# Segment sums of gathered rows: chunks in pairs of a PSUM bank, and a ring of 96 chunks

## The chip, the cores and the metric

One core of one Trainium2 chip. The time is the device time of one execution in microseconds (us), the median of several. The engines are TensorE (PE in the profile), VectorE (DVE), ScalarE (ACT), GpSimd (POOL) and SyncE (SP), which issues most transfers.

## The reference, cut to what matters

```python
# x (50000, 128) float32; src, dst (100000,), dst sorted: 50000 random edges and a loop at each node
h_self = x @ W_self.T + b_self
messages = x[src] @ W_neigh.T + b_neigh
h_neigh = segment_sum(messages, dst, num_segments=50000)
out = layernorm(x + relu(h_self + h_neigh))      # eps 1e-5, no affine part
```

The kernel sums rows of x first and multiplies once per node. An edge's loop part needs no gather, so 50,000 edges are left, and the count of a node's edges multiplies b_neigh.

## The kernel before, in words

**Lists.** The 50,000 edges that are no loops are packed in 391 chunks of 128, in the order of dst. Vector makes, from the edge lists, for each chunk the source nodes (chunk_src), the targets (chunk_dst) and the first target (first_node). They come in three parts of 99, 99 and the rest, the later two in slices between the other work (later_lists(t) of Vector): chunk_src of part 2 at t = 11 and of part 3 at t = 39. GpSimd waits for a part before it gathers from it (L466 to L475).

**Gathers.** GpSimd issues one indirect DMA a chunk (L462), in order; it brings 128 rows of x into a slot of `ring`, 84 slots. From chunk 84 on it waits (L461) until TensorE has summed triple (c - 84)//3 + 2: a triple is three chunks, and the last row block of a triple is read again by the next triple's carry matmul.

**Sums.** For a chunk Vector builds `pick` (L724), a one-hot matrix of edges by node columns; TensorE multiplies the gathered rows with it (L889), which gives the sum per node, transposed, features by nodes. A triple shares one PSUM bank of 496 columns, with chunks over columns 0 to 192, 64 to 344 and 168 to 496, so 800 columns are multiplied a triple (two matmul records in the trace for each float32 matmul). A node whose edges go on in the next triple gets the rest by a matmul of one column, the carry (L883). ScalarE copies the bank's 496 columns into `sums_t` (L990), a ring of 4096 node columns with a margin, at an offset read from a list into a register; copies overlap in columns, so each waits for the one before it. Vector joins the margin with the start at each lap (L742, L743) and clears it (L748).

**Nodes.** Nodes are worked in 131 trios of 3 x 128, counted by tau. TensorE transposes x (turn_x, L873), ScalarE copies it (L998), TensorE adds bias (L904), x times W_self + W_neigh (L908) and sums_t times W_neigh (L909) in a bank. Vector takes relu and adds x (residual, L735), and makes the statistics (L755, L763, L771, L778); ScalarE the deviation (L1007) and the scaling (L1017). SP loads x and degrees and stores the result, each with four buffers.

**Order.** Each engine has its program written out, without loops on the device. TensorE, for each t: the sums up to what sums_needed(t) says and one triple more (L946), turn_x(t + 1), products(t). products(t) waits for sums_placed, xt_copied and y_done. ScalarE, for each t: place_sums as far as TensorE sums, copy_x_t(t + 1), deviation(t - 2), normalise(t - 3). Vector, for each t: residual(t - 1), joins, the picks for t + 1, statistics, the lists. How many triples products(t) needs follows from `drift_of`, the bound on how far a chunk's first node may lie from an even spread: 768 nodes, and 384 near both ends. Inputs that break a bound go to a second, general program (check, conclude), which these inputs don't need.

Of the kernel before, what the change touches and what calls it, by code (L numbers as in the profile page):

```python
# [20 lines left out]
INT32 = mybir.dt.int32  # L21
# [4 lines left out]
P = 128  # L26
# [35 lines left out]
SPANS = ((0, 192), (64, 344), (168, 496))  # L62
SPAN = SPANS[-1][1]
PICK_AT = (0, 192, 472)
PICK = 800
# [39 lines left out]
def drift_of(triple):  # L105
    return DRIFT if TIGHT_LOW < triple < TIGHT_HIGH else TIGHT_DRIFT


def sums_needed(trio):

    return 1 + max(c for c in range(TRIOS) if P * TRIO * c - drift_of(c) < P * TRIO * (trio + 1))


def lap_joined_after(lap):

    return 1 + max(c for c in range(TRIOS) if P * TRIO * c - drift_of(c) < lap * LAP)
# [7 lines left out]
def lap_reused_from(lap):  # L124

    return -(-((lap + 1) * LAP - DRIFT - SPAN + 1) // (P * TRIO))

# [44 lines left out]
def build_common_case(nc, ctx, k, x, src, dst, out):  # L172
# [55 lines left out]
    carry = sb("carry", [P, TRIOS])  # L228
    offset_all = sb("offset_all", [1, ENTRIES // TRIO], INT32)
    offsets = sb("offsets", [1, ENTRIES // TRIO + LOAD], INT32)  # L230
# [7 lines left out]
    expected = sb("expected", [1, TRIOS])  # L238
    gap = sb("gap", [1, CHUNKS])
    faults = sb("faults", [1, 10])  # L240
# [19 lines left out]
    sum_bank, xt_bank, h_bank, list_bank = bank[0:3], bank[3:5], bank[5:7], bank[7]  # L260
# [33 lines left out]
    triples_summed = sem("triples_summed")  # L294
    sums_placed = sem("sums_placed")
    laps_joined = sem("laps_joined")
# [33 lines left out]
    with nc.Block() as block_:  # L330
# [75 lines left out]
        def _(pool):  # L406
# [8 lines left out]
            iota(columns[:], [[1, SPAN]], 0).then_inc(k.iotas, 1)  # L415
            iota(expected[:], [[TRIO * P, TRIOS]], 0).then_inc(k.iotas, 1)
# [38 lines left out]
            def gather(c):  # L455
# [4 lines left out]
                if c >= RING:  # L460
                    pool.wait_ge(triples_summed, (c - RING) // TRIO + 2)  # L461
# [16 lines left out]
        def _(dve):  # L478
# [142 lines left out]
            def spread_lists(part, t0, t1, carry0, carry1):  # L621

                c0, c1 = t0 * TRIO, t1 * TRIO
                dve.wait_ge(firsts_spread, part)
                link(v.tensor_copy(first_node[:, c0:c1], list_bank[:, 0:c1 - c0]))
                v.tensor_copy(offset_all[:, t0:t1], first_node[0:1, c0:c1:TRIO])
                v.tensor_tensor(carry[:, carry0:carry1], chunk_dst[:, carry0 * TRIO + TRIO - 1:carry1 * TRIO:TRIO],
                                first_node[:, (carry0 + 1) * TRIO:carry1 * TRIO + 1:TRIO], ALU.is_equal)
                link(v.tensor_tensor(local[:, c0:c1].rearrange("p (t q) -> p t q", q=TRIO),
                                     chunk_dst[:, c0:c1].rearrange("p (t q) -> p t q", q=TRIO),  # L630
                                     first_node[:, c0:c1:TRIO].unsqueeze(2).to_broadcast([P, t1 - t0, TRIO]), ALU.subtract))
                link(v.scalar_tensor_tensor(local[:, carry0 * TRIO + TRIO - 1:carry1 * TRIO:TRIO], carry[:, carry0:carry1], float(LAP),
                                            local[:, carry0 * TRIO + TRIO - 1:carry1 * TRIO:TRIO], ALU.mult, ALU.add))
                v.tensor_scalar(offsets[:, t0:t1], offset_all[:, t0:t1], LAP - 1, None, ALU.bitwise_and).then_inc(offsets_known, 1)
# [26 lines left out]
            spread_lists(1, 0, FIRST_TRIOS, 0, FIRST_TRIOS - 1)  # L661
# [19 lines left out]
            def check():  # L681
# [4 lines left out]
                firsts = first_node[0:1, 0:TRIOS * TRIO + 1]  # L686
                starts = firsts[:, 0:TRIOS * TRIO:TRIO]
                link(v.tensor_tensor(gap[:], firsts[:, 1:CHUNKS + 1], firsts[:, 0:CHUNKS], ALU.subtract))
                count(0, gap[:], LONGEST, ALU.is_gt)
                link(v.tensor_tensor(gap[:, 0:TRIOS - 1], firsts[:, 1:(TRIOS - 1) * TRIO:TRIO], starts[:, 0:TRIOS - 1], ALU.subtract))  # L690
                count(1, gap[:, 0:TRIOS - 1], SPANS[1][0], ALU.is_lt)
                link(v.tensor_tensor(gap[:, 0:TRIOS - 1], firsts[:, 2:(TRIOS - 1) * TRIO:TRIO], starts[:, 0:TRIOS - 1], ALU.subtract))
                count(2, gap[:, 0:TRIOS - 1], SPANS[2][0], ALU.is_lt)
                count(3, gap[:, 0:TRIOS - 1], SPANS[1][1] - 1, ALU.is_gt)
                link(v.tensor_tensor(gap[:, 0:TRIOS], firsts[:, TRIO:TRIOS * TRIO + 1:TRIO], starts, ALU.subtract))
                count(4, gap[:, 0:TRIOS], SPAN - 1, ALU.is_gt)
                link(v.tensor_tensor(gap[:, 0:TRIOS - 1], firsts[:, TRIO:(TRIOS - 1) * TRIO + 1:TRIO], firsts[:, 2:(TRIOS - 1) * TRIO:TRIO], ALU.subtract))
                count(5, gap[:, 0:TRIOS - 1], 1, ALU.is_lt)
                link(v.tensor_tensor(gap[:, 0:TRIOS], starts, expected[:], ALU.subtract))
                count(6, gap[:, 0:TRIOS], DRIFT, ALU.is_gt)  # L700
                count(7, gap[:, 0:TRIOS], -DRIFT, ALU.is_lt)
                count(8, gap[:, 0:TIGHT_LOW + 1], -TIGHT_DRIFT, ALU.is_lt)
                count(9, gap[:, TIGHT_HIGH:TRIOS], -TIGHT_DRIFT, ALU.is_lt)
                link(v.tensor_copy(unused[:, 0:10], faults[:]))
                v.reduce_sum(checks[0:1, 1:2], unused[:, 0:10], AXIS_X)
# [11 lines left out]
            def build_picks(tau):  # L717

                if tau >= DEEP:
                    dve.wait_ge(triples_summed, tau - DEEP + 1)  # L720
                for c in chunks_of(tau):
                    q = c % TRIO
                    lo, hi = SPANS[q]
                    ins = v.tensor_scalar(pick[tau % DEEP][:, PICK_AT[q]:PICK_AT[q] + hi - lo], columns[:, lo:hi],  # L724
                                          local[:, c:c + 1], None, ALU.is_equal)
                ins.then_inc(pick_built, 1)
# [54 lines left out]
            def later_lists(t):  # L781
# [13 lines left out]
                if t == 13:  # L795
                    spread_lists(2, FIRST_TRIOS, 2 * FIRST_TRIOS, FIRST_TRIOS - 1, 2 * FIRST_TRIOS - 1)
# [18 lines left out]
                if t == 41:  # L815
                    spread_lists(3, 2 * FIRST_TRIOS, ENTRIES // TRIO, 2 * FIRST_TRIOS - 1, TRIOS - 1)
# [16 lines left out]
            for t in range(TRIOS + 2):  # L833
# [22 lines left out]
        def _(pe):  # L856
# [9 lines left out]
            def turn_x(tau):  # L866
                b = tau % 2
                tiles, rows = tiles_of(tau)
                pe.wait_ge(x_landed[tau % DEEP], 16 * (tau // DEEP + 1))
                if tau >= 2:  # L870
                    pe.wait_ge(xt_copied, tau - 1)
                for q in range(tiles):
                    ins = nc.tensor.transpose(xt_bank[b][:, q * P:q * P + rows], x_in[tau % DEEP][0:rows, q, :], k.identity[0:rows, 0:rows])  # L873
                ins.then_inc(xt_turned, 1)

            def sum_chunks(tau):

                sums = sum_bank[tau % SUM_BANKS]
                pe.wait_ge(pick_built, tau + 1)
# [391 lines left out]
```

## Time and profile before

| | |
|---|---|
| median of 3 runs | 803.71 us (801.73 to 805.24) |
| the profiled execution | 807.21 us |
| its span in the profile | 805.3 us |
| mean granted TensorE clock | 0.87 of full speed |
| busy | PE 548.5, DVE 446.5, ACT 303.8, POOL 405.0 us |

The profile is of one execution. "L904" is a line of the kernel. A wait is given with what released it; "remote", or "another core or an unknown queue", stands where the trace shows no releaser, and "issue" where it shows no wait. PE is the matrix work, PEld the load of weights beside it.

### The profile page before, as it was taken

The page shows a single profiled execution, that of the slowest core. Times are in us where ns is not written, and L with a number is a line of the kernel's source. Part 1 is how long each engine was busy: PE and PEld are TensorE (multiplying, and loading weights), DVE is VectorE, ACT ScalarE, POOL GpSimd, SP SyncE. Part 2 cuts the span into 40 slices and gives each one's busy share as a digit, 9 for nine tenths or more (in the row PEclk, how much of TensorE's full clock was granted, in tenths as well). Part 3 has the DMA queues.
Part 4 walks back from the last instruction along what each step waited for, and adds up shares of the span by engine and source line. Part 5 has one row for each costly group of instructions (what it writes and reads, how often), then busy time and mean ns, then how long its engine had stood idle before and what let it go on. Part 6 is the DMA issues. An engine that isn't in the chain of part 4 may idle for free.

```text
span 805.3 us, 11397 instructions
## 1 busy us (share of the span) xinstructions
PE 548.5 (68%) x3151; PEld 434.5 (54%) x3151; DVE 446.5 (55%) x1927; ACT 303.8 (38%) x789; POOL 405.0 (50%) x424
## 2 busy tenths in 40 slices
PE   1036020118941879889678787888989798999995
PEld 0024010016730657677456576666767576778784
DVE  6783001008821768689566666675645455666765
ACT  0000000015501444446244354435445354566566
POOL 3687777731176556562756566556656566200000
PEclk9999555558985799999879999889979899999998
DMA  4222222113331435444334444434544444433333
GB/s 136 62 63 65 53 52 62 52 27 92 102 83 52 113 103 145 125 129 128 93 93 132 119 122 110 126 110 132 133 110 129 129 126 129 122 109 101 112 107 93
DMA packets 122933, 82.12 MB, mean 102 GB/s; under 512 B 15374, under 2 KB 115894, under 8 KB 122840
## 3 DMA queue, kind: packets, MB, share of 16 engines
q1 hardware_dynamic: 109208, 53.63, 23.5%
q0 software_dynamic: 13664, 27.77, 13.6%
q8 instruction: 26, 0.43, 0.2%
q14 instruction: 35, 0.29, 0.1%
HBM read 55.44 MB, written 26.71 MB: 102 GB/s over the span
## 4 chain that ended last, share of the span: by engine, by line
PE 41%; issue 21%; DVE 15%; another core or an unknown queue 11%; ACT 6%; POOL 4%; DMA 2%; ACTq 1%; DVEq 0%; POOLq 0%
PE bank L889 17%; PE bank L908 8%; PE bank L909 7%; DVE pick L724 4%; PE bank L873 4%; ACT result L1017 3%; PE bank L904 3%; DVE y L735 2%; PE bank L883 2%; DVE stats L755 2%; ACT sums_t L990 1%; POOL ring L462 1%; DMA dst_block<-in_dst,block_index 1%; POOL dst_block L422 1%
## 5 line engine op out<-in xcount | busy, mean ns | idle before, releaser
L462 POOL DMA_INDIRECT ring<-in_x,chunk_src x391 | 379.9, 972 | 265.7 <-issue 110.2
L990 ACT COPY sums_t<-bank 128x496 f32 x131 | 74.9, 572 | 415.5 <-remote 223.1
L889 PE MATMUL bank<-pick,ring 128*128 128x192 f32 (+2 forms) x782 | 227.6, 431 | 2.4 <-DMA ring<-in_x,chunk_src 2.4
L908 PE MATMUL bank<-wsum_t,x_t 128*128 128x128 f32 (+1 forms) x782 | 173.2, 304 | 11.7 <-issue 11.5
L735 DVE SCALAR_TENSOR_TENSOR y<-bank,x_in 128x384 f32<-128x384 f32 x131 | 72.5, 554 | 191.5 <-PE bank L909 73.9
L909 PE MATMUL bank<-wn_t,sums_t 128*128 128x128 f32 (+1 forms) x782 | 158.6, 284 | 19.4 <-issue 19.4
L1017 ACT ACTIVATE result<-y,minus_mean,rstd 128x128 f32<-128x128 f32 x391 | 163.4, 486 | 0.0
L889 PEld LDWEIGHTS bank<-pick,ring 128*128 128x128 f32 x782 | 142.5, 205 | 17.1 <-DMA ring<-in_x,chunk_src 1.9
L908 PEld LDWEIGHTS bank<-wsum_t,x_t 128*128 128x128 f32 (+1 forms) x782 | 124.8, 200 | 37.7 <-issue 37.7
L909 PEld LDWEIGHTS bank<-wn_t,sums_t 128*128 128x128 f32 (+1 forms) x782 | 125.5, 201 | 18.9 <-issue 18.9
L724 DVE TENSOR_SCALAR pick<-columns,local 128x192 f32<-128x192 f32 (+2 forms) x391 | 118.0, 357 | 0.2
L883 PE MATMUL bank<-carry,ring 128*128 128x1 f32 x260 | 43.6, 237 | 86.4 <-DVE pick L724 62.9
L883 PEld LDWEIGHTS bank<-carry,ring 128*128 128x128 f32 x260 | 41.9, 201 | 98.4 <-DVE pick L724 71.6
L904 PE MATMUL bank<-bias,degrees_t 12*128 12x384 bf16 x131 | 45.4, 346 | 71.5 <-issue 61.2
L771 DVE RECIPROCAL rstd<-std 128x3 f32<-128x3 f32 x131 | 21.9, 167 | 127.5 <-issue 75.1
L755 DVE BATCH_NORM_STATS2 stats<-y 128x6 f32<-128x128 f32 x391 | 87.4, 278 | 0.2
L998 ACT COPY x_t<-bank 128x384 f32<-128x384 f32 x131 | 63.1, 482 | 61.7 <-PE bank L873 34.8
L873 PE MATMUL bank<-identity,x_in 128*128 128x128 f32 x391 | 70.3, 289 | 18.8 <-issue 18.8
L873 PEld LDWEIGHTS bank<-identity,x_in 128*128 128x128 f32 x391 | 54.8, 150 | 49.5 <-issue 24.4
L904 PEld LDWEIGHTS bank<-bias,degrees_t 12*128 12x128 bf16 x131 | 12.0, 91 | 99.0 <-issue 98.8
L1007 ACT ACTIVATE std<-mean_var,eps 128x3 f32<-128x3 f32 x131 | 40.2, 307 | 0.4 <-DVE mean_var L763 0.4
L763 DVE BATCH_NORM_AGGREGATE mean_var<-stats 128x2 f32<-128x6 f32 x391 | 38.9, 155 | 0.0
(122 smaller groups left out, 208.8 us busy)
## 6 DMA issues: line engine op xcount, KB each, us to landing
x_in<-in_x SPq DMA_DIRECT2D x130, 192.0 KB
out<-result SPq DMA_DIRECT2D x130, 192.0 KB
ring<-in_x,chunk_src POOLq DMA_INDIRECT x391
degrees_t<-degrees_dram SPq DMA_DIRECT2D x130, 2.2 KB
dst_padded<-in_dst SPq DMA_DIRECT2D x1, 390.6 KB
src_padded<-in_src SPq DMA_DIRECT2D x1, 390.6 KB
edge_src<-in_src SPq DMA_DIRECT2D x1, 390.6 KB
edge_dst<-in_dst SPq DMA_DIRECT2D x1, 390.6 KB
```

What stands on the lines that cost most here:

```text
L462: nc.gpsimd.indirect_dma_start(ring[:, c % RING, :], None, x, bass.IndirectOffsetOnAxis(ap=chunk_src[:, c:c + 1], axis=0)).then_inc(gather ...
L724: ins = v.tensor_scalar(pick[tau % DEEP][:, PICK_AT[q]:PICK_AT[q] + hi - lo], columns[:, lo:hi], local[:, c:c + 1], None, ALU.is_equal)
L735: v.scalar_tensor_tensor(y[tau % DEEP][0:rows, 0:tiles, :], h_bank[b][0:rows, 0:tiles * DIM].rearrange("p (q d) -> p q d", q=tiles), 0.0, ...
L755: ins = v.bn_stats(stats[b][0:rows, q, :], y[b][0:rows, q, :])
L873: ins = nc.tensor.transpose(xt_bank[b][:, q * P:q * P + rows], x_in[tau % DEEP][0:rows, q, :], k.identity[0:rows, 0:rows])
L883: mm(sums[:, 0:1], ring[:, (tau * TRIO - 1) % RING, :], carry[:, tau - 1:tau], start=True, stop=False, skip_group_check=True)
L889: ins = mm(sums[:, lo:hi], ring[:, c % RING, :], pick[tau % DEEP][:, PICK_AT[q]:PICK_AT[q] + hi - lo], start=(tau == 0 and q == 0), stop=( ...
L904: mm(h_bank[b][0:rows, 0:tiles * DIM], degrees_t[tau % DEEP][:, 0:rows], k.bias[:, 0:tiles, :], start=True, stop=False)
L908: mm(h, x_t[b][:, q, 0:rows], k.wsum_t[:], start=False, stop=False)
L909: ins = mm(h, sums_t[:, at:at + rows], k.wn_t[:], start=False, stop=(q == tiles - 1))
L990: nc.scalar.copy(sums_t[:, bass.ds(at, SPAN)], sum_bank[tau % SUM_BANKS][:, 0:SPAN]).then_inc(sums_placed, 1)
L1017: ins = nc.scalar.activation(result[b][0:rows, q, :], y[b][0:rows, q, :], ACT.Identity, bias=minus_mean[b][0:rows, q:q + 1], scale=rstd[b] ...
```

## The change

A chunk now has 193 columns of its own, at its own offset, and two chunks lie side by side in one bank: columns 0 to 192 and 192 to 384, the shared column 192 being the first of the second chunk. An edge whose target is the next chunk's first node goes to column 192 of its chunk. The second chunk's last column (384) is added to the first column of the next chunk in sums_t by an activation of ScalarE with that column as its bias, after the next chunk's copy. The carry matmul is gone, but not `carry`, from which `local` is made. Picks are three of 194 columns a trio. place_sums runs once a chunk (391 times) and copies 192 columns; register loads bring 8 offsets each. The ring of gathered rows has 96 slots, and gather c waits for chunks_summed of c - 95, so that chunk c - 96 has been summed; each chunk's matmul increments that semaphore. Four banks hold sums, one holds transposed x (before three and two), so turn_x waits for the copy of the transposes before. The sums run ahead of products(t) by what it needs and at least two chunks more, in whole pairs. The drift bounds are 640, 384 and 192 nodes. The margin of sums_t is 192 columns. The checks on the lists are changed to match.

```diff
-SPANS = ((0, 192), (64, 344), (168, 496))
-SPAN = SPANS[-1][1]
+SPAN = 192
+PAIR = 2
...
-MARGIN = 512
+MARGIN = SPAN
...
-DRIFT = 768
+DRIFT = 640
 TIGHT_DRIFT = 384
-TIGHT_LOW = 14
-TIGHT_HIGH = 117
-
-RING = 84
+END_DRIFT = 192
+TIGHT_CHUNKS = 42
+END_CHUNKS = 9
+
+RING = 96
 GATHER_SEMS = 8
-SUM_BANKS = 3
-LOAD = 4
+SUM_BANKS = 4
+LOAD = 8
...
+def drift_of(chunk):
+    from_end = min(chunk, CHUNKS - chunk)
+    return END_DRIFT if from_end <= END_CHUNKS else TIGHT_DRIFT if from_end <= TIGHT_CHUNKS else DRIFT
+
+def chunks_starting_below(node):
+    return 1 + max(c for c in range(CHUNKS) if P * c - drift_of(c) < node)
+
+def whole_pairs(chunks):
+    return min(CHUNKS, -(-chunks // PAIR) * PAIR)
 
 def sums_needed(trio):
-    return 1 + max(c for c in range(TRIOS) if P * TRIO * c - drift_of(c) < P * TRIO * (trio + 1))
+    return chunks_starting_below(P * TRIO * (trio + 1))
+
+def sums_ahead(trio):
+    return whole_pairs(sums_needed(min(trio, TRIOS - 1)) + PAIR)
...
-    columns = sb("columns", [P, SPAN])
+    columns = sb("columns", [P, SPAN + 2])
...
-    pick = [sb(f"pick{i}", [P, PICK]) for i in range(DEEP)]
+    pick = [sb(f"pick{i}", [P, TRIO, SPAN + 2]) for i in range(DEEP)]
...
-    sum_bank, xt_bank, h_bank, list_bank = bank[0:3], bank[3:5], bank[5:7], bank[7]
+    sum_bank, xt_bank, h_bank, list_bank = bank[0:4], bank[4], bank[5:7], bank[7]
...
                 if c >= RING:
-                    pool.wait_ge(triples_summed, (c - RING) // TRIO + 2)
+                    pool.wait_ge(chunks_summed, c - RING + 1)
...
-                link(v.scalar_tensor_tensor(... float(LAP), ... ALU.mult, ALU.add))
+                link(v.scalar_tensor_tensor(local[:, r0:r1], carry[:, r0:r1], float(SPAN), local[:, r0:r1], ALU.mult, ALU.max))
...
                 if tau >= DEEP:
-                    dve.wait_ge(triples_summed, tau - DEEP + 1)
+                    dve.wait_ge(chunks_summed, TRIO * (tau - DEEP + 1))
                 for c in chunks_of(tau):
...
+                    ins = v.tensor_scalar(pick[tau % DEEP][:, c % TRIO, :], columns[:], local[:, c:c + 1], None, ALU.is_equal)
...
-                while built < min(TRIOS, sums_needed(min(t + 1, TRIOS - 1)) + 1):
+                while built * TRIO < sums_ahead(t + 1):
...
-                if tau >= 2:
-                    pe.wait_ge(xt_copied, tau - 1)
+                if tau >= 1:
+                    pe.wait_ge(xt_copied, tau)
...
-            def sum_chunks(tau):
...
-                if tau:
-                    mm(sums[:, 0:1], ring[:, (tau * TRIO - 1) % RING, :], carry[:, tau - 1:tau], start=True, stop=False, skip_group_check=True)
...
+            def sum_chunk(c):
+                tau = c // TRIO
+                if c % TRIO == 0:
+                    pe.wait_ge(pick_built, tau + 1)
+                    pe.wait_ge(gathered[tau % GATHER_SEMS], gathers_upto(tau))
+                frame = SPAN * (c % PAIR)
+                into = sum_bank[c // PAIR % SUM_BANKS]
+                if c % PAIR == 0 and c // PAIR >= SUM_BANKS - 1:
+                    pe.wait_ge(sums_placed, PAIR * (c // PAIR + 2 - SUM_BANKS))
+                ins = mm(into[:, frame:frame + SPAN + 1], ring[:, c % RING, :], pick[tau % DEEP][:, c % TRIO, 0:SPAN + 1],
+                         start=(c % PAIR == 0), stop=True, skip_group_check=True)
+                ins.then_inc(chunks_summed, 1)
...
-                while summed < min(TRIOS, sums_needed(t) + 1):
-                    sum_chunks(summed)
+                while summed < sums_ahead(t):
+                    sum_chunk(summed)
...
+            def place_sums(c):
+                if c % LOAD == 0:
+                    load_offsets(c)
+                at = act.snap(held[c % LOAD], min_val=0, max_val=LAP - 1)
+                if c % PAIR == 0:
+                    act.wait_ge(chunks_summed, min(c + PAIR, CHUNKS))
...
+                    act.wait_ge(sums_placed, c)
...
+                frame = SPAN * (c % PAIR)
+                whole = sum_bank[c // PAIR % SUM_BANKS]
+                copied = nc.scalar.copy(sums_t[:, bass.ds(at, SPAN)], whole[:, frame:frame + SPAN])
+                if c > 0 and c % PAIR == 0:
+                    copied.then_inc(frames_copied, 1)
+                    act.wait_ge(frames_copied, c // PAIR)
+                    nc.scalar.activation(sums_t[:, bass.ds(at, 1)], sum_bank[(c // PAIR - 1) % SUM_BANKS][:, PAIR * SPAN:PAIR * SPAN + 1],
+                                         ACT.Identity, bias=sums_t[:, bass.ds(at, 1)], scale=1.0).then_inc(sums_placed, 1)
+                else:
+                    copied.then_inc(sums_placed, 1)
...
-                while placed < min(TRIOS, sums_needed(min(t, TRIOS - 1)) + 1):
+                while placed < sums_ahead(t):
```

## Rows read from the trace of the kernel before

**Rows 1.** The page's busy times: us, share of the span, instructions.

```profile
PE 548.5 (68%) x3151; PEld 434.5 (54%) x3151; DVE 446.5 (55%) x1927; ACT 303.8 (38%) x789; POOL 405.0 (50%) x424
```

**Rows 2.** Stretches, L904: length, busy us (and instructions) on PE and weight load, clock, DMA.

```profile
184.30:218.40 34.10, 2.71 (x8) 0.73 (x8) 0.93 0.38 106
...
218.40:259.40 41.00, 0.86 (x3) 0.28 (x3) 0.73 0.26 71
...
382.10:691.50 309.40, 21.17 (x61) 5.55 (x61) 0.91 0.44 119
...
691.50:805.30 113.80, 9.85 (x30) 2.72 (x30) 0.98 0.38 107
```

**Rows 3.** Stretches, L462 on POOL: length, busy us (gathers), clock, DMA share, GB/s.

```profile
218.40:259.40 41.00, 31.12 (x33) 0.73 0.26 71
...
382.10:691.50 309.40, 185.80 (x193) 0.91 0.44 119
```

**Rows 4.** Timeline, 606 to 612: start, us taken, engine, line, form [idle before].

```profile
606.43 0.39 PE L909 MATMUL bank<-wn_t,sums_t 128*128 128x128 f32 x2
...
606.80 1.59 PE L889 MATMUL bank<-pick,ring 128*128 128x192 f32 x6
...
608.00 0.94 POOL L462 DMA_INDIRECT ring<-in_x,chunk_src  x1 [0.30 <-issue]
...
610.48 0.56 DVE L735 SCALAR_TENSOR_TENSOR y<-bank,x_in 128x384 f32<-128x384 f32 x1 [3.29 <-remote]
...
610.65 0.57 ACT L990 COPY sums_t<-bank 128x496 f32 x1 [2.76 <-remote]
...
611.31 1.05 POOL L462 DMA_INDIRECT ring<-in_x,chunk_src  x1 [2.37 <-remote]
```

**Rows 5.** POOL's waits, 382 to 691.5: us in total, times, longest.

```profile
POOL ring L462 <- remote: 47.1, 22, 4.4
...
POOL ring L462 <- PE bank L889: 24.6, 12, 4.7
```

**Rows 6.** Timeline of PE in the tail, one trio.

```profile
718.10 0.28 PE L883 MATMUL bank<-carry,ring 128*128 128x1 f32 x2
...
718.24 1.59 PE L889 MATMUL bank<-pick,ring 128*128 128x192 f32 x6
...
719.67 0.49 PE L873 MATMUL bank<-identity,x_in 128*128 128x128 f32 x3
...
720.09 0.33 PE L904 MATMUL bank<-bias,degrees_t 12*128 12x384 bf16 x1
...
721.80 0.28 PE L883 MATMUL bank<-carry,ring 128*128 128x1 f32 x2
```

**Rows 7.** Timeline of ACT in the tail, one trio.

```profile
719.95 0.57 ACT L990 COPY sums_t<-bank 128x496 f32 x1 [1.41 <-PE bank L889]
720.42 0.49 ACT L998 COPY x_t<-bank 128x384 f32<-128x384 f32 x1
720.79 0.31 ACT L1007 ACTIVATE std<-mean_var,eps 128x3 f32<-128x3 f32 x1
720.98 1.25 ACT L1017 ACTIVATE result<-y,minus_mean,rstd 128x128 f32<-128x128 f32 x3
```

**Rows 8.** Forms of ACT in the tail, and of DVE: busy us, mean ns, idle before.

```profile
L1007 ACT ACTIVATE std<-mean_var,eps 80x1 f32<-80x1 f32 x1 | 0.3, 280 | 0.0
...
L998 ACT COPY x_t<-bank 128x80 f32<-128x80 f32 x1 | 0.2, 210 | 0.0
...
L742 DVE TENSOR_TENSOR sums_t<-sums_t 128x512 f32<-128x512 f32 x12 | 8.3, 688 | 13.7 <-ACT sums_t L990 13.7
...
L743 DVE MEMSET sums_t<- 128x512 f32 x12 | 5.8, 485 | 2.1 <-DVE sums_t L742 1.6 <-issue 0.5
```

**Rows 9.** Timeline: the gathers after two stops, and PE before the first.

```profile
181.34 0.57 PE L909 MATMUL bank<-wn_t,sums_t 128*128 128x128 f32 x1 [0.34 <-issue]
...
184.33 0.94 POOL L462 DMA_INDIRECT ring<-in_x,chunk_src  x1 [14.75 <-remote]
...
382.17 0.94 POOL L462 DMA_INDIRECT ring<-in_x,chunk_src  x1 [12.67 <-DVE chunk_dst L657]
```

More of the change, by code:

```diff
@@ L102, in gnn_kernel @@
             build_general_case(nc, general, weights, x, src, dst, out)
-def drift_of(triple):
-    return DRIFT if TIGHT_LOW < triple < TIGHT_HIGH else TIGHT_DRIFT
+def drift_of(chunk):
[5 more added lines that the diff above has]
+    return min(CHUNKS, -(-chunks // PAIR) * PAIR)
 def sums_needed(trio):
-    return 1 + max(c for c in range(TRIOS) if P * TRIO * c - drift_of(c) < P * TRIO * (trio + 1))
+    return chunks_starting_below(P * TRIO * (trio + 1))
+def sums_ahead(trio):
+    return whole_pairs(sums_needed(min(trio, TRIOS - 1)) + PAIR)
 def lap_joined_after(lap):
-    return 1 + max(c for c in range(TRIOS) if P * TRIO * c - drift_of(c) < lap * LAP)
+    return chunks_starting_below(lap * LAP)
 def lap_read_by(lap):
@@ L124, in lap_reused_from @@
 def lap_reused_from(lap):
-    return -(-((lap + 1) * LAP - DRIFT - SPAN + 1) // (P * TRIO))
+    return -(-((lap + 1) * LAP - DRIFT - SPAN + 1) // P)
 class Constants:
@@ L227, in build_common_case @@
     local = sb("local", [P, ENTRIES])
-    carry = sb("carry", [P, TRIOS])
-    offset_all = sb("offset_all", [1, ENTRIES // TRIO], INT32)
-    offsets = sb("offsets", [1, ENTRIES // TRIO + LOAD], INT32)
+    carry = sb("carry", [P, ENTRIES])
+    offset_all = sb("offset_all", [1, ENTRIES], INT32)
+    offsets = sb("offsets", [1, ENTRIES + LOAD], INT32)
     raw_at = sb("raw_at", [SPREAD, WINDOW])
@@ L691, in check @@
[L691 to L696, printed above, removed]
@@ L866, in turn_x @@
             def turn_x(tau):
[L867 removed]
                 tiles, rows = tiles_of(tau)
                 pe.wait_ge(x_landed[tau % DEEP], 16 * (tau // DEEP + 1))
[L870 to L871 removed]
+                if tau >= 1:
+                    pe.wait_ge(xt_copied, tau)
                 for q in range(tiles):
[L873 removed]
+                    ins = nc.tensor.transpose(xt_bank[:, q * P:q * P + rows], x_in[tau % DEEP][0:rows, q, :], k.identity[0:rows, 0:rows])
                 ins.then_inc(xt_turned, 1)
[L876 to L891 removed]
+            def sum_chunk(c):
[10 more added lines that the diff above has]
+                ins.then_inc(chunks_summed, 1)
             def products(tau):
@@ L972, in place_sums @@
[L972 to L978 removed]
+                act.load(held[:], offsets[:, c:c + LOAD])
+            def place_sums(c):
[4 more added lines that the diff above has]
+                    act.wait_ge(chunks_summed, min(c + PAIR, CHUNKS))
+                if c == 0:
@@ L988, in place_sums @@
                 if free_of >= 0:
                     act.wait_ge(h_done, free_of + 1)
-                nc.scalar.copy(sums_t[:, bass.ds(at, SPAN)], sum_bank[tau % SUM_BANKS][:, 0:SPAN]).then_inc(sums_placed, 1)
+                frame = SPAN * (c % PAIR)
[8 more added lines that the diff above has]
+                    copied.then_inc(sums_placed, 1)
```

93 lines of the change are left out of this document (32 added, 61 removed).

## The prediction, made before the changed kernel was run

> **What bounds the kernel now.** I read the page's shares first, then the span in stages, then one stretch of each kind. The page shows no full engine: TensorE is busy 68%, GpSimd 50%, ScalarE 38% [rows 1]. So no share settles it, and a saving on one engine buys nothing by itself.
>
> Cut at GpSimd's gathers, the span shows three kinds of stage. The number of bias matmuls (L904, one per trio) against the number of gathers tells them apart [rows 2, 3]:
> - GpSimd runs without a stop. In 218.4 to 259.4 it issues 33 gathers and TensorE starts 3 trios. The stretch before the first stop is alike.
> - GpSimd is held by the ring. In 382.1 to 691.5 there are 193 gathers and 61 trios, 5.07 us a trio; the stretch from 259 to the wait for the third list is of this kind too.
> - GpSimd is idle: 30 trios in the last 113.8 us, and 8 in 184.3 to 218.4, where it waits for the second list.
>
> Why the middle stage is slow shows at 606 to 612 [rows 4]. The products end at 606.82, but Vector's residual, which waits for them, starts at 610.48. The sums end at 608.39 and ScalarE's copy starts at 610.65. GpSimd has ended its last allowed gather at 608.94 and resumes at 611.31, 2.37 later. So the consumers hear of TensorE's work late, about 1.5 us after GpSimd has stopped, and all at once. I cannot name the mechanism from the trace; I take the pattern: while gathers run one behind the other, what TensorE has finished is seen late, and a stop of GpSimd frees it. In the middle stage there are 34 such stops, 71.7 us, so 2.1 us each and 5.7 gathers between two [rows 5]. A gather takes 0.94 us and has 0.30 before it, 1.25 from start to start [rows 4], so a stop costs 1.8 us more than going on. That is cheap: 1.8 us of a stopped GpSimd lets TensorE do nearly two trios, which in the tail take 7.4 us.
>
> With GpSimd idle the beat is 3.70 us, and it is TensorE's: carry 0.14, sums 1.43, transposes 0.42, bias and products 1.71 (from the starts at 718.10, 718.24, 719.67, 720.09 and 721.80) [rows 6]. ScalarE waits 1.41 of it [rows 7].
>
> **TensorE's saving.** Sums go from 800 columns to 3 x 193 = 579 a trio: 1.43 x 579/800 = 1.03, and the carry's 0.14 goes. 3.70 becomes 3.17. Where TensorE doesn't set the beat this is worth nothing.
>
> **ScalarE's cost.** One copy of 496 columns becomes three of 192 and, for each pair, one add of a column. Each waits for the one before it, and the add for its copy. A copy of 192 lies between the 0.21 us of 80 columns and the 0.49 of 384, 0.31 us on that line [rows 7, 8]. The one-column activation with a bias pointer from PSUM isn't in the trace; the 80x1 activation takes 280 ns [rows 8], and the 128x128 with two pointers 0.48 (three in 1.25, from start to start 0.385) [rows 7]; I take 0.28, the nearest form. From a releasing instruction's end to the next copy takes 0.12 us (the sums end at 719.83, the copy starts at 719.95) [rows 6, 7]. So 3 x 0.43 + 1.5 x 0.40 = 1.89 us. The rest of its trio is 1.73: 0.37 from the copy of x to the deviation, 0.19 to the scaling, and 1.16, three by 0.385, for that [rows 7]. Less 0.1 of overlap, ScalarE needs 3.5 us a trio, more than TensorE's 3.17. Ends: 3.25 if the waits cost 0.07, 3.9 if the add costs 0.48 and the waits 0.15. So the idle-GpSimd beat becomes 3.5, not 3.17: a gain of 0.18 us.
>
> The Trainium skill (ScalarE: Activation LUTs, What ACT_TABLE_LOAD costs) gives 186 ns and 0.833 ns an element with immediates, and 93 ns more for a pointer. By it the copy is 0.35, the add 0.28, and the beat an estimated 3.6; the sum would rise by about 6 us.
>
> **The ring.** It grows from 84 to 96 chunks, and its release is finer. Gather c now waits for chunk c-96; before, since a trio's last row was also read by the next trio's carry, it waited for triple (c-84)/3+2. The last gather (390) needs 104 triples summed before, 312 chunks, and 295 chunks after. The lookahead of the sums is 4 triples before (L946) and 3t+10 chunks, rounded up to a pair, after. So GpSimd ends when trio 100 is in work before (which the counts bear out: 30 bias matmuls are left after 691.5 [rows 2]) and trio 95 after. Gather 197 allows trio 35 before, 31 after. A longer lead is not a gain here: GpSimd has the same 391 gathers to issue at 1.25, and every trio put off until it is idle costs 3.5, where in the middle stage it costs only its share of a stop, 1.8/2.
>
> Step by step, against the profiled execution (807.21 us, span 805.3, which lies 0.4% over the median 803.71):
> - First list: the 14.75 us stop at gather 96 goes [rows 9], but then GpSimd waits for the second list, which needs Vector at t = 11. TensorE came free 12 us after the last gather (169.58, and 181.91 for the last of the products) [rows 9]; three more gathers put that off by 4 us. Bounds 0 and +8, I take +2.
> - Second list: 8 trios at 3.5 for 3.7: -1.4.
> - To gather 198: 4.3 trios fewer are worked before it, 2.2 stops less, -4.3. Then GpSimd waits for the third list, which Vector makes at t = 39: 12.67 us now [rows 9], and 4.3 x 3.5 = 15.1 more, less 0.6 for the quicker beat. Together +10.2.
> - Middle stage: 5 trios fewer, 2.6 stops: -4.7.
> - Tail: 5 trios more at 3.5, +17.6; 30 trios by 0.18 less, -5.5; 12.1 together.
> - Laps' joins: 512 to 192 columns, 0.69 us for the add of each of 12 [rows 8]; perhaps 0.1 us a lap is seen, -1.
>
> Sum: 2 - 1.4 + 10.2 - 4.7 + 12.1 - 1 = +17 us. That gives 824 for a profiled execution, and **821 us** against the median.
>
> Nothing: the picks (582 columns for 800) can only shorten Vector's part, which is hidden by its waits; without that cover the sign is still a gain. One transpose bank for two: its copy is done a whole trio before. The lists' larger spread is some columns more, beside the gathers; if seen, under 1 us. Loads of offsets, one per 8 chunks: beside the scaling; without that cover 0.3 us each, already in the upper beat. SP's queue and GpSimd's issues keep their number; SP's loads and stores wait for the same events. ScalarE's scaling stands behind the longer placing, and the store behind that, with four buffers between.
>
> **Rivals.**
> 1. *More chunks per stop, and TensorE's beat* (the other side). The release is by chunk and TensorE's trio is shorter, so a third trio may fit between two stops. Some 208 chunks are worked in ring-held stages; at 8 a stop for 5.7 that is 208 x 1.8 x (1/5.7 - 1/8) = 19 us less, 802. If the chain on ScalarE also hides, 51 trios (35 + 8 + 8) run at 3.17: another 17, 785. For: TensorE's two trios take 7.4 us of the 9.5 between two restarts of GpSimd (7.5 for six gathers, 2.1 for the stop), so it has room. Against: products need the pair just summed in every other trio, where before they needed only the trio before. It decides from 8 chunks a stop together with a beat under 3.4. Chance 0.25 for 775 to 799, 0.11 for one half of it, near 803.
> 2. *Fewer chunks per stop.* If the pair that products need is heard only at a stop, GpSimd stops every 4 chunks: 208 x 1.8 x (1/4 - 1/5.7) = +28, 849. Chance 0.08.
> 3. *ScalarE's chain at its upper bound*: 3.9 by 51 trios, +20, 841. It's part of my case's range.
> 4. *TensorE's bound everywhere*: 131 x 0.53 = 69 us less, 735. The middle stage, in which TensorE is not the limit, speaks against it: 0.02, within the 0.25.
>
> **How the numbers follow.** My case (lead dearer than the beat's gain) has 0.56 and spans 806 to 845; with rival 2, slower by over 0.5%, which is about what a measurement of this kernel can tell from no change, gets 0.64. Faster 0.25, within 0.5% 0.11. The range reaches from most of rival 1 to the lower part of rival 2: 784 to 848. My own case's stands above.
>
> **What would show it.** Right: the last gather issued near 695 to 702 with 34 to 36 trios left; a wait of 25 to 30 us before gather 198; L883 gone, sums of a trio near 1.03 us at full clock; in the tail a beat of 3.4 to 3.6, ScalarE without idle time and TensorE waiting for sums_t. Wrong: a tail beat of 3.2 with ScalarE idle; a wait before gather 198 no longer than 15 us; stops in the middle stage fewer than 20 or more than 45.

## The result, and the profile after

| | before | changed |
|---|---|---|
| median of 4 runs | 804.48 us (801.73 to 806.39) | 817.24 us (814.21 to 821.50) |
| ratio, 95% interval | | 1.0178 [1.0138, 1.0218] |
| the profiled execution, its span | 807.21, 805.3 us | 817.83, 815.9 us |
| mean granted TensorE clock | 0.87 | 0.82 |

The change made the kernel 1.8% slower, which is clear of the spread of the runs; 821.0 was predicted, in a range of 784 to 848. Medians and ratios are of fast runs: two of e4's four runs (733.73 and 734.53 us) were in a slower state and are left out. In the changed kernel L478 is the gather, L887 the sums, L991 the copy of a chunk's columns, L995 the added column, L902 the bias matmul (one per trio), L1006, L1015 and L1025 ScalarE's other three steps, L744 and L745 the laps' join.

The page's busy times and groups of the changed kernel (busy us, mean ns | idle before), which answer to [rows 1]:

```profile
PE 480.2 (59%) x2891; PEld 401.4 (49%) x2891; DVE 418.6 (51%) x1919; ACT 397.9 (49%) x1244; POOL 407.4 (50%) x424
...
L991 ACT COPY sums_t<-bank 128x192 f32 x391 | 124.1, 317 | 318.9 <-remote 202.5
L887 PE MATMUL bank<-pick,ring 128*128 128x193 f32 x782 | 171.8, 353 | 55.0 <-issue 41.8
...
L995 ACT ACTIVATE sums_t<-bank,sums_t 128x1 f32 x195 | 51.0, 261 | 6.3
```

TensorE lost 68 us of work and ScalarE gained 94, and the time moved by 13: busy times settle nothing here. The stretches do, cut at GpSimd's stops as in [rows 2, 3]. First L902: length, busy us (and instructions) on PE and on the weight load, granted clock, DMA share, GB/s.

```profile
221.00:281.20 60.20, 1.13 (x3) 0.28 (x3) 0.58 0.25 71
...
396.70:691.70 295.00, 19.79 (x55) 5.06 (x55) 0.85 0.43 118
691.70:815.90 124.20, 11.48 (x35) 3.19 (x35) 0.97 0.41 115
```

In 221.0 to 281.2 GpSimd issues 48 gathers without a stop, and TensorE starts 3 trios. The middle stage has the same 193 gathers as before, with 55 trios for 61. The last gather goes at 691.7, as before, but 35 trios are left instead of 30. GpSimd's timeline at the two list waits and at the end (start, us taken, engine, line, form, [idle before]), which answers to [rows 9]:

```profile
221.05 0.94 POOL L478 DMA_INDIRECT ring<-in_x,chunk_src  x1 [47.80 <-DVE chunk_dst L669]
...
396.77 0.95 POOL L478 DMA_INDIRECT ring<-in_x,chunk_src  x1 [30.41 <-DVE chunk_dst L669]
...
691.69 0.95 POOL L478 DMA_INDIRECT ring<-in_x,chunk_src  x1 [0.30 <-issue]
```

The first list wait, 47.80, stands where there were two before: the stop of 14.75 at gather 96 and one of 30.46 for the list, so the stop only moved. The wait before gather 198 was 12.67. So of the span's 10.6 us more, 14.6 were there by gather 198 (396.8 against 382.2), the middle stage gave 14.4 back (295.0 against 309.4), and the tail took 10.4 more (124.2 against 113.8). GpSimd's waits in the middle stage (us in total, times, longest), which answer to [rows 5]:

```profile
POOL ring L478 <- PE bank L887: 34.6, 25, 2.7
...
POOL ring L478 <- remote: 26.7, 21, 2.1
```

61.3 us in 46 stops, 1.33 each, for 71.7 in 34, 2.1 each. Above the ordinary gap of 0.30 that is 0.25 us per gather ((61.3 - 46 x 0.30)/193), for 0.32 before. The stops come more often and are cheaper. (The counts go by the releaser that the trace names, and some of these waits are of the ordinary length. Counted by length, over 0.36 us, there are 43 stops of 1.42 us for 37 of 2.06: six more, not twelve.)

ScalarE in the tail, for two trios (the last lines of the second, from its fourth copy on, are left out), which answers to [rows 7]:

```profile
730.32 0.31 ACT L991 COPY sums_t<-bank 128x192 f32 x1
730.66 0.26 ACT L995 ACTIVATE sums_t<-bank,sums_t 128x1 f32 x1
731.03 0.32 ACT L991 COPY sums_t<-bank 128x192 f32 x1
731.25 0.48 ACT L1006 COPY x_t<-bank 128x384 f32<-128x384 f32 x1
731.62 0.31 ACT L1015 ACTIVATE std<-mean_var,eps 128x3 f32<-128x3 f32 x1
731.82 1.26 ACT L1025 ACTIVATE result<-y,minus_mean,rstd 128x128 f32<-128x128 f32 x3
732.97 0.30 ACT L991 COPY sums_t<-bank 128x192 f32 x1
733.31 0.26 ACT L995 ACTIVATE sums_t<-bank,sums_t 128x1 f32 x1
733.68 0.32 ACT L991 COPY sums_t<-bank 128x192 f32 x1
734.15 0.32 ACT L991 COPY sums_t<-bank 128x192 f32 x1 [0.15 <-ACT sums_t L991]
734.50 0.26 ACT L995 ACTIVATE sums_t<-bank,sums_t 128x1 f32 x1
...
736.81 0.30 ACT L991 COPY sums_t<-bank 128x192 f32 x1
```

It is idle for 0.15 us in 6.49, where it waited 1.41 in 3.70. The trios alternate: one has two copies and an add and takes ScalarE 2.65 (730.32 to 732.97), the other four and two and takes 3.84 (to 736.81). TensorE's side of the same trios, which answers to [rows 6]:

```profile
731.41 1.47 PE L887 MATMUL bank<-pick,ring 128*128 128x193 f32 x8
732.73 0.49 PE L874 MATMUL bank<-identity,x_in 128*128 128x128 f32 x3
733.72 0.32 PE L902 MATMUL bank<-bias,degrees_t 12*128 12x384 bf16 x1 [0.50 <-ACT sums_t L995]
...
735.41 0.82 PE L887 MATMUL bank<-pick,ring 128*128 128x193 f32 x4
...
736.49 0.33 PE L902 MATMUL bank<-bias,degrees_t 12*128 12x384 bf16 x1
...
740.21 0.32 PE L902 MATMUL bank<-bias,degrees_t 12*128 12x384 bf16 x1 [0.22 <-ACT sums_t L995]
```

From one bias matmul to the next it is 2.77 us where two chunks are summed between (TensorE's own time) and 3.72 where four are (it waits for ScalarE's add). Over the tail, without its last two intervals (which have no work of other trios in them), the mean is 3.38. The joins fell as their columns did (busy us, mean ns; groups of DVE by line), for 688 and 485 in [rows 8]:

```profile
L744 DVE TENSOR_TENSOR sums_t<-sums_t 128x192 f32<-128x192 f32 x12 | 4.3, 359 | 8.7 <-ACT sums_t L995 5.6 <-issue 3.1
L745 DVE MEMSET sums_t<- 128x192 f32 x12 | 2.6, 218 | 1.3
```

### The profile page after: what moved, and what is told of

The parts are those of the page before. It is cut to its first block, busy times and chain, and to the rows that moved or that the text cites. A ratio compares the mean times of both kernels' runs of the same rounds, so it can differ in the third digit from the quotient of the medians.

```text
span 815.9 us, 12095 instructions
## 1 busy us (share of the span) xinstructions
PE 480.2 (59%) x2891; PEld 401.4 (49%) x2891; DVE 418.6 (51%) x1919; ACT 397.9 (49%) x1244; POOL 407.4 (50%) x424
## 4 chain that ended last, share of the span: by engine, by line
PE 29%; another core or an unknown queue 27%; ACT 16%; issue 12%; DVE 8%; POOL 3%; ACTq 2%; DMA 2%; DVEq 0%; POOLq 0%
PE bank L887 9%; PE bank L906 8%; PE bank L907 6%; ACT result L1025 6%; ACT sums_t L991 5%; PE bank L874 3%; PE bank L902 3%; ACT sums_t L995 2%; DVE pick L727 2%; ACT x_t L1006 1%; ACT std L1015 1%; DVE y L737 1%; DMA dst_block<-in_dst,block_index 1%; ACTq L988 1%
## 5 line engine op out<-in xcount | busy, mean ns | idle before, releaser
L478 POOL DMA_INDIRECT ring<-in_x,chunk_src x391 | 383.1, 980 | 262.6 <-issue 101.2
L991 ACT COPY sums_t<-bank 128x192 f32 x391 | 124.1, 317 | 318.9 <-remote 202.5
L887 PE MATMUL bank<-pick,ring 128*128 128x193 f32 x782 | 171.8, 353 | 55.0 <-issue 41.8
L906 PE MATMUL bank<-wsum_t,x_t 128*128 128x128 f32 (+1 forms) x782 | 181.7, 318 | 0.0
L887 PEld LDWEIGHTS bank<-pick,ring 128*128 128x128 f32 x782 | 137.0, 207 | 65.6 <-issue 49.6
L907 PE MATMUL bank<-wn_t,sums_t 128*128 128x128 f32 (+1 forms) x782 | 166.8, 298 | 0.3 <-issue 0.3
L1025 ACT ACTIVATE result<-y,minus_mean,rstd 128x128 f32<-128x128 f32 x391 | 163.4, 486 | 0.0
L906 PEld LDWEIGHTS bank<-wsum_t,x_t 128*128 128x128 f32 (+1 forms) x782 | 132.4, 212 | 26.6 <-issue 26.6
L907 PEld LDWEIGHTS bank<-wn_t,sums_t 128*128 128x128 f32 (+1 forms) x782 | 134.1, 215 | 0.0
L902 PE MATMUL bank<-bias,degrees_t 12*128 12x384 bf16 x131 | 46.2, 353 | 143.2 <-issue 98.8
L727 DVE TENSOR_SCALAR pick<-columns,local 128x194 f32<-128x194 f32 x391 | 103.3, 320 | 0.2
L1006 ACT COPY x_t<-bank 128x384 f32<-128x384 f32 x131 | 63.1, 481 | 68.5 <-remote 36.1
L902 PEld LDWEIGHTS bank<-bias,degrees_t 12*128 12x128 bf16 x131 | 12.0, 92 | 169.6 <-issue 169.4
L995 ACT ACTIVATE sums_t<-bank,sums_t 128x1 f32 x195 | 51.0, 261 | 6.3
L1015 ACT ACTIVATE std<-mean_var,eps 128x3 f32<-128x3 f32 x131 | 40.2, 307 | 0.0
L597 DVE COPY_PREDICATED words<-moves,words 99x311 int32<-99x311 int32 (+15 forms) x48 | 27.2, 566 | 1.1
```

The costliest lines, as they stand in the source:

```text
L478: nc.gpsimd.indirect_dma_start(ring[:, c % RING, :], None, x, bass.IndirectOffsetOnAxis(ap=chunk_src[:, c:c + 1], axis=0)).then_inc(gather ...
L727: ins = v.tensor_scalar(pick[tau % DEEP][:, c % TRIO, :], columns[:], local[:, c:c + 1], None, ALU.is_equal)
L887: ins = mm(into[:, frame:frame + SPAN + 1], ring[:, c % RING, :], pick[tau % DEEP][:, c % TRIO, 0:SPAN + 1], start=(c % PAIR == 0), stop=T ...
L902: mm(h_bank[b][0:rows, 0:tiles * DIM], degrees_t[tau % DEEP][:, 0:rows], k.bias[:, 0:tiles, :], start=True, stop=False)
L906: mm(h, x_t[b][:, q, 0:rows], k.wsum_t[:], start=False, stop=False)
L907: ins = mm(h, sums_t[:, at:at + rows], k.wn_t[:], start=False, stop=(q == tiles - 1))
```

## The experiments

The prediction claims two things: the longer lead of the gathers (more slots, and release by chunk) costs more than the rest of the change brings, and with GpSimd idle the chain on ScalarE eats most of what TensorE saves. The experiments ran in four groups, each with the kernel before on the same chip, and each ratio below is to that one: 804.24 us (e1 to e4), 581.2 (e5 to e7), 803.58 (e8 to e10), 808.78 (e11, e12). The 581.2 is a matter of its own, told below, and e5 to e7 aren't in the table. The columns on gathers and trios are read from one trace of each kernel (e4's is of its run of 733.73 us); gather 198 is left out where no wait for a list stands before it.

| kernel | slots, release | gather 198 at | last gather | trios left | rest of the span | median us | ratio |
|---|---|---|---|---|---|---|---|
| before | 84, triple | 382.2 | 691.5 | 30 | 113.8 | 804.48 | |
| e3 | 96, triple | 400.3 | 701.7 | 34 | 131.3 | 834.73 | 1.038 |
| changed | 96, chunk | 396.8 | 691.7 | 35 | 124.2 | 817.24 | 1.018 |
| e8, the same again | 96, chunk | 397.5 | 698.3 | 35 | 123.5 | 823.78 | 1.024 |
| e9, e8 without the add | 96, chunk | 394.2 | 689.1 | 35 | 115.0 | 805.82 | 1.004 |
| e1 | 79, chunk | 374.2 | 673.2 | 29 | 104.0 | 777.39 | 0.967 |
| e2 | 48, chunk | | 649.6 | 19 | 70.1 | 719.00 | 0.893 |
| e4 | 48, triple | | 663.4 | 18 | 68.5 | 724.99 | 0.902 |
| e11 | 24, chunk | | 669.3 | 10 | 39.9 | 710.14 | 0.881 |
| e12 | 12, chunk | | 668.6 | 6 | 25.6 | 698.06 | 0.867 |

**e1: the changed kernel with the old lead.** With 79 slots and release by chunk, the last gather needs 312 chunks summed, the same as before.

```diff
-RING = 96
+RING = 79
```

> The changed kernel with 79 slots in the ring instead of 96, nothing else. With a release by chunk this gives the last gather the same lead as the kernel before (312 chunks summed). Theory (a longer lead costs, since trios put off until GpSimd is idle cost a full beat): 5.7 trios fewer stand behind the last gather, 5.7 x 3.38 = 19 us less tail; the wait before gather 198 falls from 30 to about 11 us; about 8 us more in stops. Together -30 us: 787, under the kernel before. Rival (the change's loss is ScalarE's longer placing, and the ring is neutral): within 5 us of the changed kernel's 817. Second rival (a longer lead helps, as it saves stops): 825.

777.39 us, 0.9665 [0.9624, 0.9705]: 40 us under the changed kernel, where 30 was expected. So at the old lead everything else in the change is worth 27 us, and the seventeen slots cost 40. (Two gathers in three wait in e1 for one or two chunks more than in the kernel before, so its lead is shorter by one chunk in the mean; at 40 us for seventeen that is an estimated 2 of the 27.) The stretches of e1 (L902), cut at gather 198 and at the last:

```profile
374.10:673.30 299.20, 21.45 (x61) 5.61 (x61) 0.89 0.45 125
673.30:777.20 103.90, 9.54 (x29) 2.65 (x29) 0.94 0.41 114
```

The 28 us of span less than before lie in all three parts: 8 by gather 198 (374.2 for 382.2), 10 in the middle stage, 10 in the tail. The terms of the prediction that have nothing to do with the lead add up to 8.5 (1.4, 0.6, 5.5 and 1).

**e3: the kernel before with 96 slots,** and nothing else.

```diff
-RING = 84
+RING = 96
```

> The kernel before with 96 slots instead of 84: the ring's part of the change alone. Theory: 4 trios more behind the last gather and behind gather 197, 2 x 4 x 3.7 = 30 us more, less 8 us of stops: 826. Rival (the ring is neutral or helps): 804 or less.

834.73 us (826 expected), 1.0381 [1.0339, 1.0422]: 30 us slower, by a longer prefetch alone. GpSimd's waits of e3 up to the last gather:

```profile
POOL ring L462 <- DVE chunk_dst L657: 78.1, 2, 49.7
POOL ring L462 <- remote: 59.5, 25, 7.9
POOL ring L462 <- PE bank L889: 28.0, 18, 3.5
```

The two waits for lists are 49.7 and 28.4 us. In its tail 34 trios are left and the bias matmuls stand 3.70 apart, TensorE's beat as before. This is the prediction's mechanism by itself: the same gathers are issued, and the trios that were put off are worked one by one while GpSimd has nothing to do.

**e2 and e4: both kernels with 48 slots.**

In e2, the changed kernel (in e4, the kernel before, the old value is 84):

```diff
-RING = 96
+RING = 48
```

> The changed kernel with 48 slots. Theory: GpSimd is held by the ring from gather 48 on, both list waits vanish, and the tail falls to some 19 trios: 47 us ahead of the first gather, 489 us of gathers, 81 us of stops, 68 us of tail, 685 us, between 650 and 715. Rival (the ring neutral): 817. Second rival (a short ring starves TensorE, since gathers land late or the lists come late): over 817.

> The kernel before with 48 slots. Theory: as for the changed kernel with 48, with stops of 2.1 us and a tail beat of 3.7: 47 + 489 + 110 + 66 = 712 us, between 680 and 740. Rival (neutral): 804. It also says whether the changed kernel is the faster one once the lead is short: by theory it is, by some 25 us.

719.00 us, 0.8932 [0.8888, 0.8975], and 724.99 us (of two runs), 0.9022 [0.8967, 0.9076]. The direction held and the size fell short: a little over the range in e2, within it in e4. The other half of e4's expectation missed: with 48 slots the changed kernel was to be faster by some 25 us, and it is by 6, with intervals that overlap. So what the rest of the change is worth isn't a fixed sum; it depends on the ring it stands beside. GpSimd's waits of e2:

```profile
POOL ring L478 <- PE bank L887: 84.2, 58, 3.1
POOL ring L478 <- remote: 43.6, 29, 8.5
```

No wait for a list is left (78 us in the changed kernel), but the stops are 127.8 us in 87, where I had expected 81. Less 26 for the ordinary gaps, that is 0.26 us per gather over all 391, the price per gather of the changed kernel's middle stage. It is now paid from the first stop to the end. The span falls by 96 us: 42 before the last gather (649.6 for 691.7) and 54 in the tail.

**e5 to e7: a chip on which the kernel before takes 581 us.** e5 leaves out the add of a pair's last column (the sums of the nodes at a pair's end lack it), e6 is the changed kernel with 24 slots, e7 replaces the indirect gathers by plain transfers of 128 rows (the sums are of other rows; what the gathers bring is left out).

```diff
-                if c > 0 and c % PAIR == 0:
-                    copied.then_inc(frames_copied, 1)
...
-                                         ACT.Identity, bias=sums_t[:, bass.ds(at, 1)], scale=1.0).then_inc(sums_placed, 1)
-                else:
-                    copied.then_inc(sums_placed, 1)
+                copied.then_inc(sums_placed, 1)
```

```diff
-                nc.gpsimd.indirect_dma_start(ring[:, c % RING, :], None, x,
-                                             bass.IndirectOffsetOnAxis(ap=chunk_src[:, c:c + 1], axis=0)
+                nc.gpsimd.dma_start(ring[:, c % RING, :], x[P * min(c, TILES - 2):P * min(c, TILES - 2) + P, :]
                                     ).then_inc(gathered[tau % GATHER_SEMS], 16)
```

> The changed kernel with the add of a pair's last column left out (those nodes' sums lack a part); 96 slots. Theory (with GpSimd idle the beat alternates between TensorE's and ScalarE's, and the chain of copies and adds is what keeps it at 3.38 us instead of 3.17): 1.5 x 0.38 us of ScalarE go per trio, the tail's beat falls to TensorE's, 2.8 to 3.2 us, over some 51 trios that are worked while GpSimd is idle: 10 to 15 us less, 802 to 807. Rival (the chain is hidden, the beat is TensorE's own): within 3 us of 817.

> The changed kernel with 24 slots. Theory (only the lead and the stops count): against 48 slots the tail is 8 trios shorter, 8 x 3.2 = 26 us, with 24/4.6 = 5 stops more of 1.2 us, 6 us: 719 - 20 = 699. Rival (with so few slots the time from a gather's issue to its landing, or the pairs' grain, starves TensorE): over 719.

> The changed kernel with each gather replaced by a plain transfer of 128 rows of x of the same size, issued by GpSimd too (so the sums are of other rows). It asks what delays the hearing of TensorE's work. If the indirect gathers' descriptors on GpSimd do it, the late starts and the stops' 1.2 us vanish, TensorE works through the early stretch, and the time falls well under 750. If it is GpSimd's issuing of any transfer, or the traffic itself, it stays above 790.

567.31 us (0.9781 [0.9733, 0.9829]), 570.52 (0.9818 [0.9768, 0.9867]) and 542.67 (one run). The sums behind the expectations of e5 and e6 don't apply, since the stages they were made for don't exist there. The stretch of e6 (24 slots) from 221.0 to 281.2, first the bias matmuls, then the gathers:

```profile
221.00:281.20 60.20, 4.96 (x15) 1.36 (x15) 1.00 0.56 150
...
221.00:281.20 60.20, 46.48 (x46) 1.00 0.56 150
```

46 gathers go out one behind the other, and 15 trios start beside them, where the changed kernel on its chip started 3 beside 48. GpSimd's waits of e6 for the ring are all of the ordinary length:

```profile
POOL ring L478 <- issue: 85.3, 280, 0.3
POOL ring L478 <- PE bank L887: 33.8, 111, 0.3
```

Even with 24 slots it never stops: TensorE keeps up beside the gathers, and GpSimd's 391 gathers at 1.25 us set the end (last gather at 548.7 with 24 slots and, in e5 with 96, at 545.7). So the lead has next to no price on that chip. The unedited changed kernel and the kernel before weren't compared there. The questions of e5 and e6 were put again where the kernel before takes over 800 us.

**e8 and e9: the changed kernel again, and without the add.**

> The changed kernel itself, once more, since in the last three runs the kernel before took 581 us instead of 804, with no late starts behind the gathers: a chip on which what the prediction read at 606 us isn't there. If this run finds the kernel before at 804, the ratio is 1.016 again. If it finds it at 581, GpSimd's 391 gathers of 1.25 us set the end of both (47 + 489 + 30 us), the lead has no price, and the ratio is between 0.975 and 1.0. Rival for that case: the finer work of the changed kernel costs on ScalarE, 1.01.

> The changed kernel without the add of a pair's last column, beside the changed kernel. Where late starts are there: the tail's beat falls from 3.38 to 2.8 to 3.2 us, 802 to 807 against 817. Where they are not: GpSimd sets the end, so within 2 us of the changed kernel.

823.78 us, 1.0242 [1.0211, 1.0273], and 805.82 us, 1.0044 [1.0011, 1.0076]. The verdict on the change repeats, at 6 us more. The add and the wait for the copy before it cost 18 us (10 to 15 expected): without them the whole change is worth next to nothing in time. The tails of e8 and e9 (L902), two kernels that differ in this alone:

```profile
698.40:821.80 123.40, 11.31 (x35) 3.19 (x35) 0.98 0.42 115
```

```profile
689.20:804.10 114.90, 11.47 (x35) 3.18 (x35) 0.98 0.44 122
```

8.5 us of the 18 are here, 0.24 a trio, and TensorE's beats in e9 are 2.79 and 3.43 in turn, its own. The other 9 lie ahead of the last gather, where GpSimd is held less: its idle time before gathers is 263.8 us in e9 and 271.2 in e8.

**e10: plain transfers, where the kernel before takes 803.58 us.** The edit is that of e7.

> The changed kernel with each gather replaced by a plain transfer of 128 rows issued by GpSimd. Where late starts are there, this asks what makes them: with the indirect gathers as their cause the time falls well under 750; with any issuing on GpSimd or the traffic as the cause it stays above 790. Where they are not there, it repeats 543.

541.75 us, one run, against 823.78 for the changed kernel on that chip, and the same as e7 on the quick one. What separates the two chips is gone with the indirect form. The stretch of e10 from 127 to 152, bias matmuls (L901 here), then the transfers (L478):

```profile
127.00:152.00 25.00, 2.31 (x7) 0.63 (x7) 1.00 0.79 228
...
127.00:152.00 25.00, 25.00 (x48) 1.00 0.79 228
```

48 transfers in 25 us, each 0.53 us on GpSimd and none with a gap between, at 228 GB/s, and 7 trios start beside them (3.6 us each) at full clock. So neither a GpSimd that is never idle nor the traffic holds TensorE's results back. A copy starts on time there. The timeline of e10 at 128:

```profile
128.18 0.59 PE L886 MATMUL bank<-pick,ring 128*128 128x193 f32 x2 [0.18 <-DVE pick L726]
...
128.89 0.32 ACT L990 COPY sums_t<-bank 128x192 f32 x1 [0.47 <-PE bank L886]
```

0.12 us from the end of the sums to the copy, as in the tail, while transfers run. e10 also shortens GpSimd's own instruction from 0.94 to 0.53 us and reads 128 neighbouring rows in place of scattered ones, so it doesn't say which part of the indirect form does the harm.

**e11 and e12: 24 and 12 slots.**

In e11 (in e12 the new value is 12):

```diff
-RING = 96
+RING = 24
```

> The changed kernel with 24 slots, a second time, for a chip with the late starts: 24/48 slots there by theory 20 us less than the 719 with 48 slots, 699; by the rival (landing time or the pairs' grain starve TensorE) over 719. On a chip without them (kernel before at 581) 570 again.

> The changed kernel with 12 slots. Where late starts are there, theory takes another 4 trios off the tail and adds 3 stops, 699 - 9 = 690; but a gather issued 12 chunks ahead is only some 14 us ahead of its use and a stop takes 2 us, so here the rival has its best chance: TensorE waits for landings, and the time rises over the 24-slot one. Where they are not there: within 5 us of 570.

710.14 us, 0.8806 [0.8732, 0.8879], and 698.06 us, 0.8672 [0.8606, 0.8737]. The changed kernel with 12 slots is by 12 us the fastest with indirect gathers where the kernel before takes over 800, and beats both kernels by over 100. The rival, that a short ring starves TensorE and raises the time, doesn't show down to 12 slots. The last stretch of e12, after its last gather (L902):

```profile
668.70:694.20 25.50, 1.88 (x6) 0.56 (x6) 0.94 0.35 100
```

Below 48 slots the gathers end later (669 for 650), because the waits grow from 127.8 us to 151.8 (24 slots) and 145.7 (12), but six trios are left for the end instead of 19. GpSimd's waits of e12:

```profile
POOL ring L478 <- PE bank L887: 94.7, 64, 3.3
...
POOL ring L478 <- remote: 51.0, 36, 2.4
```

## Why the prediction was right, and which term was off

**The lead, as predicted.** 35 trios were left at the last gather (34 to 36 said), and it went at 691.7, 3 us ahead of the window of 695 to 702 (698.3 in e8). The wait before gather 198 was 30.4 us, where 25 to 30 was said. That the lead causes it is shown from both sides: e3 adds it alone and loses 30 us, e1 takes it away alone and gains 40.

**The middle stage is the mis-sized term.** I had 4.7 us less for five trios and 2.6 stops fewer. It was 14.4 less, with six trios fewer and more stops, not fewer. (In e8, the same kernel on another chip, the stage took 300.8, so several us of this are spread between runs.) The step that failed is "a stop costs 1.8 us more than going on", a price I held fixed: a stop took 1.33 us instead of 2.1 (1.42 for 2.06 by length). Waits with a named releaser, or a remote one, fell by 10.4 us (71.7 to 61.3), the gaps without one by 6.4 (51.8 to 45.4), and the gathers themselves took 2.5 more (185.8 to 188.3). e1 and e3 show two parts: 10.2 us come with everything but the lead (299.2), for which my sum had nothing in this stage, and 7.8 with the lead alone (301.6). Why the stops are shorter isn't shown. The release by chunk alone doesn't account for it: e1 has it too, and its stops by length are 35 of 1.83 us.

The 46 stops also fell just past the 45 that I had named as a sign against me (43 by length). Rival 1 looked for its gain in more chunks per stop (8 for 5.7). They became fewer, 4.2, and rival 2 wanted 28 us for that. Both had the count as the cost, and the length decided. Both were also priced over 208 chunks; the changed kernel issues 244 gathers in stretches held by the ring (51 from 281.2 to 396.7, and 193), which makes the 19 us of rival 1 22, and the 28 of rival 2 33.

**To gather 198: 14.6 for 10.8.** The first list wait ended 2.6 us later, and the gathers up to 197 then took 5.7 less (366.4 for 369.5), about the 4.3 foreseen for stops (2.2 stops at 1.8 are 4.0; the 4.3 was a slip). The wait for the third list grew by 17.7 where 14.5 was in the sum.

**The tail: 10.4 for 12.1.** Five trios more, and a mean beat of 3.38 for my 3.5. TensorE's own beat was about right: 3.11 in e9, where 3.17 was said. In the term for ScalarE the waits were too dear: from start to start a copy takes 0.34 and an add 0.37, so three and one and a half come to 1.58, not 1.89, and the last copy doesn't hold up the copy of x for longer than 0.22. The rest was right (731.25 to 732.97 is 1.72, 1.73 said). The copy takes 317 ns (0.31 said) and the add 261 (0.28). The 0.3 us for a load of offsets that nothing covers came from no row. In this trace it is about 0.7: where a chunk whose number is a multiple of 8 is the second pair's first in a heavy trio (every 24th chunk), the idle time before its copy is 0.83 us instead of 0.15. The structure held too: ScalarE without idle time, TensorE waiting for sums_t. One thing I missed: an even trio and an odd one differ. TensorE sets the light one (2.77), ScalarE the heavy one (3.72 to 4.03, for TensorE's own 3.43). A mean per engine hides that the slower engine changes from trio to trio.

The Trainium skill (ScalarE: Activation LUTs, What ACT_TABLE_LOAD costs) has figures from which the copy was estimated at 0.35, the add at 0.28 and the beat at 3.6. The trace has 0.317, 0.261 and 3.38: these two instructions are below the page's figures, and the measured ones decide.

**The right total came from two terms that were both too small.** The parts that have nothing to do with the lead were to bring 8.5 us, and e1 shows 27. The lead was then to cost 25.5, and it cost 30 (e3, at 84 to 96 and by triple) to 40 (changed against e1). The two errors have opposite signs and nearly cancel: 13 us measured, 17 predicted. That the lead outweighs the rest was the reason given, and it holds; that the sum came within 4 us was luck. Nor do the two parts simply add: at 48 slots the rest of the change brought 6 us (e2 and e4), not 27.

**The short rings came out slower than expected** (719 for 685, 710 for 699, 698 for 690). It is one term, the stops. With 48 slots they took 127.8 us where 81 was said; with 24 slots 24 us more, where 6 was said. That is 0.26 to 0.31 us per gather over the whole run. The step to 12 slots was right: 12 us less, 9 said.

## What to carry to other kernels

A prefetch ring has a price when issuing the prefetch holds back those who consume it: work that could go on beside the issue is put off until the issuing engine is idle, and then has a tail of its own. Before a ring is made longer, count how many units of work are left when the last prefetch is issued, and time a much shorter ring (here 12 slots for 96 was worth 119 us, on chips where the issue does hold them back). And where a change makes the lead longer along with other things, measure the lead apart: here the lead was worth +40 us and the rest -27, and together they looked like +13.

## What was not expected of the hardware

The same kernel took 581 us in one group of runs and 804 to 809 in the other four groups; kernels of a group share a chip. The slow time goes with the late starts of [rows 4], which the quick chip doesn't have. In the changed kernel TensorE started 3 trios beside 48 gathers and in e6, on the quick chip, 15 beside 46. With plain transfers from the same queue the effect is absent on a slow chip too (541.75 us for 823.78, one run), at 228 GB/s and over twice the rate of issue. That much is shown.

What the prediction called it, "what TensorE has finished is seen late", is only part of it. TensorE's own instructions come late as well. These are matmuls of one trio of the kernel before, at the end of the long run of gathers; between them `products` waits for nothing:

```profile
173.64 0.37 PE L909 MATMUL bank<-wn_t,sums_t 128*128 128x128 f32 x1 [2.75 <-issue]
175.73 0.37 PE L908 MATMUL bank<-wsum_t,x_t 128*128 128x128 f32 x1 [1.72 <-issue]
177.83 0.37 PE L908 MATMUL bank<-wsum_t,x_t 128*128 128x128 f32 x1 [1.73 <-issue]
```

The last of this trio's matmuls starts at 181.34, 12 us after the last gather had ended. In the changed kernel four sums stand 2.1, 3.5 and 2.1 us apart from 245.06 to 252.77, where the tail's come every 0.37 or less, and then TensorE does nothing for 21 us while GpSimd goes on issuing. ScalarE's results, by contrast, are seen in time in the same stretch: Vector's step after the deviation that ends at 238.76 starts at 238.79. The trace calls TensorE's gaps "issue", so it doesn't say whether the matmuls, their completion or the supply of TensorE's instructions is held up.

Why indirect gathers do it, whether it is their descriptors, the 128 offsets read from memory, the scattered rows or the length of the instruction, and what differs between the chips, stays open. Gathers spaced apart by a pause, or of another size, were not tried. The granted clock is lower too where TensorE is nearly idle (a mean of 0.58 in the changed kernel's stretch, 1.00 in e6's); what that adds by itself was not measured.
